# An eight-batch attention and feed-forward kernel on one core: odd pairs' reciprocals first in place 3, 512 KB transfers at other places, and the feed-forward part's first input taken as a ninth attention input

## What is computed

```python
x = x + _layernorm(_L0_attn_ref(_layernorm(x), w_q, w_kv, w_out, b_out, scale))   # 16 heads of 64
x = x + _layernorm(_L0_ffn_ref(_layernorm(x), w1, s1, w2, s2, h1, t1, h2, t2, w3, s3))

# attention: q, k of each head have their length set to 1; sim = exp(scale) * q k^T; softmax; times v; times w_out
# feed-forward: h = silu(x w1 * s1) * (x w2 * s2); h = gelu(h h1 * t1); h = gelu(h h2 * t2); h w3 * s3
```

## Time and profile before

| | us |
|---|---|
| median of three runs | 1770.43 |
| range of the three | 1767.59 to 1770.76 |
| the profiled execution, device time | 1771.34 |
| its span, first to last instruction | 1769.3 |
| attention: first scores to last scores (slots 0 to 255) | 35.4 to 1087.8 |
| first feed-forward matmul | 1104.2 |
| mean granted clock of TensorE | 0.991 |

### The profile page before, as it was taken

The page is one execution under the profiler, slowest core; times in us unless marked ns, Lnnn a source line. Parts: engine busy times, 40 slices in busy tenths (PEclk is TensorE's granted clock), DMA queues, the critical chain, the costliest instruction groups (busy, mean ns, idle before and its releaser), DMA issues.

```text
span 1769.3 us, 24636 instructions
## 1 busy us (share of the span) xinstructions
PE 1702.5 (96%) x8578; PEld 1421.8 (80%) x8578; DVE 1179.0 (67%) x2026; ACT 1010.0 (57%) x1350; POOL 463.4 (26%) x557
## 2 busy tenths in 40 slices
PE   5999999999999999999999998999999999999998
PEld 4778888888878887887888776888888888888887
DVE  5777877877877877877877775545454545445454
ACT  4876776877777776876877775323223231323231
POOL 3423543543533543543543331000000000000000
PEclk9999999999999999999999998999999999999999
DMA  4555556556656655655555665300000000000000
GB/s 132 128 127 142 128 134 146 128 134 146 138 126 144 137 132 138 137 129 130 114 116 130 160 150 127 140 12 4 22 24 1 25 1 24 1 24 1 24 1 24
DMA packets 76636, 162.89 MB, mean 92 GB/s; under 512 B 28256, under 2 KB 28640, under 8 KB 76512
## 3 DMA queue, kind: packets, MB, share of 16 engines
q1 hardware_dynamic: 67008, 127.59, 31.7%
q10 hardware_dynamic: 8496, 30.03, 5.7%
q0 software_dynamic: 1008, 3.67, 0.5%
HBM read 68.44 MB, written 20.19 MB: 50 GB/s over the span
## 4 chain that ended last, share of the span: by engine, by line
PE 78%; DVE 7%; DMA 5%; issue 4%; ACT 3%; POOL 1%; SPq 0%; ACTq 0%; DVEq 0%; POOLq 0%
PE bank L1059 16%; PE pair L1136 13%; PE pair L1137 12%; PE bank L1001 12%; PE bank L1073 5%; PE pair L1042 4%; PE pair L1043 4%; PE pair L1126 3%; PE pair L1127 3%; DVE Pl L716 2%; DMA work<-rows 2%; PE bank L1028 2%; DMA rows<-Rp 2%; PE bank L1153 2%; PE bank L1154 2%
## 5 line engine op out<-in xcount | busy, mean ns | idle before, releaser
L1059 PE MATMUL bank<-Ph,V 128*128 128x512 f32 x1024 | 371.1, 403 | 30.4 <-DVE Pl L716 29.1
L1136 PE MATMUL pair<-hh,f 128*128 128x512 f32 x1024 | 399.3, 390 | 0.7 <-DVE hl L829 0.2
L1137 PE MATMUL pair<-hl,f 128*128 128x512 f32 x1024 | 398.6, 389 | 0.0
L493 ACT ACTIVATE P<-pair,sh 128x1024 f32<-128x1024 f32 x256 | 286.5, 1119 | 179.0 <-PE pair L1043 145.9
L716 DVE TENSOR_TENSOR Pl<-P,Ph 128x1024 fp32r<-128x1024 f32 x256 | 314.2, 1227 | 1.4 <-ACT Ph L498 1.2
L550 ACT ACTIVATE hr<-pair,ct 128x512 f32<-128x512 f32 x128 | 88.3, 690 | 357.7 <-PE pair L1137 357.7
L1001 PE MATMUL bank<-w,xh 128*128 128x256 f32 (+1 forms) x1024 | 284.8, 340 | 5.5 <-DVE qk L695 2.3
L498 ACT ACTIVATE Ph<-P 128x1024 fp32r<-128x1024 f32 x256 | 271.8, 1062 | 8.1
L1059 PEld LDWEIGHTS bank<-Ph,V 128*128 128x128 f32 x1024 | 195.5, 191 | 92.6 <-issue 45.9
L1136 PEld LDWEIGHTS pair<-hh,f 128*128 128x128 f32 x1024 | 192.2, 188 | 43.8 <-DVE hl L829 3.4
L1137 PEld LDWEIGHTS pair<-hl,f 128*128 128x128 f32 x1024 | 192.2, 188 | 39.7
(11 more groups left out here) (104 smaller groups left out, 2652.0 us busy)
## 6 DMA issues: line engine op xcount, KB each, us to landing
stack<-turned SPq DMA_DIRECT2D x128, 384.0 KB, 4.4
stack<-turned SPq DMA_DIRECT2D x128, 256.0 KB, 4.7
work<-rows SPq DMA_DIRECT2D x128, 128.0 KB, 3.0
raw<-in_h ACTq DMA_DIRECT2D x16, 512.0 KB, 3.8
xr<-in_h ACTq DMA_DIRECT2D x16, 512.0 KB, 4.8
f<-raw ACTq DMA_DIRECT2D x12, 512.0 KB, 6.4
f<-raw SPq DMA_DIRECT2D x10, 512.0 KB, 7.5
xt<-in_x SPq DMA_DIRECT2D x8, 512.0 KB, 4.1
```

The costliest lines, as they stand in the source:

```text
L493: e.activation(M.P[:, i % 2, :], M.SB[i % 2][:, :], ACT.Exp, bias=M.sh[:, h:h + 1]).then_inc(S["exp"])
L1059: d = e.matmul(M.OB[:, :], v, p[:, u % 3, j * 512:(j + 1) * 512], start=jt == 0 and m == 0, stop=jt == 3 and m == 2)
L1136: e.matmul(ps, w, M.hh[src][:, k, :].bitcast(to), start=k == 0, stop=False)
L1137: d = e.matmul(ps, w, M.hl[src][:, k, :].bitcast(to), start=False, stop=k == KH - 1)
```

## The change

- **VectorE, place 3.** `invert` for odd pairs stands ahead of `p_low` instead of at the end of the slot. At place 7 it stays at the end.
- **VectorE, places 0 and 1.** `turn_low` for odd pairs moves from the end of place 0 to place 1, behind that slot's `p_low`.
- **VectorE, slot 21.** `normal` stands ahead of the second `x_low` and of `turn_low` instead of behind them.
- **Transfers.** The copies move from place 3 to place 7. The looks of slots 20 and 28 move to 21 and 29. `load_x` moves from slot 27 to slot 31, `load_xr` from 0 to 6 of the next batch, and `store_x1` ahead of the stack transfers of its slot. `LOADS` stays.
- **The flag.** `count_all` moves from slot 226 to 225, `flag_sum` on TensorE from 226 to 229, and `flag` from 227 to 230. `bank_plan` gives other banks from there on.
- **The ninth input.** The first feed-forward input goes the way of a batch's attention input: loaded at slot 223 into `xt`, normalized at slots 227 to 236 with half of that on GpSimd, transposed at 243 and 244, split at 245. The separate steps in slots 246 to 253 go. The tiles `xn`, `xh3`, `xl3` become the same memory as `xt`, `xh`, `xl`. The load of `xv` for the first batch moves behind the slots, to SyncE.

```diff
-FLAG_AT, BRANCH_AT = 226, NU - 1
+FLAG_AT, BRANCH_AT = 229, NU - 1
...
-LOOKS = (16,) + tuple(32 * b + r for b in range(7) for r in (20, 24, 28))
+LOOKS = (16,) + tuple(32 * b + r for b in range(7) for r in (21, 24, 29))
...
 def copy_at(i):
...
-    n, r = divmod(i - 11, 8)
+    n, r = divmod(i - 15, 8)
...
+        if 0 <= pb < B - 1 and i32_ == 16:
+            store_x1(pb)
         if pair_of(i) is not None:
             stack(pair_of(i), 0)
...
-        if b + 2 < B and i32_ == 27:
+        if b + 2 <= B and i32_ == 31:
             load_x(b + 2)
-        if i and i32_ == 0:
+        if 0 <= pb and i32_ == 6:
             load_xr(pb)
+    load_xv(0)
     load_xv(1)
...
-        if i == NU - 10:
-            load_xv0()
...
-        early = i % 4 == 1 and i32_ != 21
...
+        if r == 3 and 0 <= n - 2 < NP:
+            invert(n - 2)
         if 0 <= i - 1 < NU:
             p_low(i - 1)
+        if r == 1 and pair_of(i - 1) is not None:
+            turn_low(pair_of(i - 1), 1)
+            turn_low(pair_of(i - 1), 0)
...
-        if early and 0 <= n - 3 < NP:
+        if i % 4 == 1 and 0 <= n - 3 < NP:
             normal(n - 3)
...
-        if i % 4 == 1 and not early and 0 <= n - 3 < NP:
-            normal(n - 3)
-        if i % 4 == 3 and 0 <= n - 2 < NP:
+        if r == 7 and 0 <= n - 2 < NP:
             invert(n - 2)
...
-        if i == FLAG_AT:
+        if i == FLAG_AT - 4:
             count_all()
...
-        if i in (NU - 8, NU - 7):
-            norm3(0, 2 * (i - NU + 8))
-            norm3(0, 2 * (i - NU + 8) + 1)
...
-        if i // 32 + 1 < B and i % 32 in (19, 20):
+        if i < NU and i % 32 in (19, 20):
             x_turn(i // 32 + 1, i % 32 - 19)
-        if i == NU - 3:
-            turn3(0)
...
+        M.xn, M.xh3, M.xl3 = M.xt, M.xh, M.xl
```

More of the change, by code:

```diff
@@ L98, in bank_plan @@
             order += [(("y", 2 * quad_of(i)), i), (("y", 2 * quad_of(i) + 1), i)]
-        if b + 1 < B and i % 32 in (19, 20):
+        if b < B and i % 32 in (19, 20):
             order.append((("x", 2 * (b + 1) + i % 32 - 19), i))
-        if i == NU - 3:
-            order += [(("x3", 0), i), (("x3", 1), i)]
         if i == FLAG_AT:
@@ L140, in wait_bank @@
         elif kind == "x3":
-            q.wait_ge("xh3", n + 1)
-            q.wait_ge("xl3", n + 1)
+            q.wait_ge("xh3", n - 1)
+            q.wait_ge("xl3", n - 1)
     return bank
@@ L227, in load_x @@
             q.wait_ge("xT", 2 * b)
-        e.dma_start(M.xt[:, :, :], M.x[b]).then_inc(S["x"], 16)
+        if b == B:
+            q.wait_ge("x1", 16)
+        e.dma_start(M.xt[:, :, :], M.x[b] if b < B else M.x1[0]).then_inc(S["x"], 16)
     def load_wo(k):
@@ L408, in pool_program @@
         i32_, pb = i % 32, i // 32 - 1
-        if b + 1 < B and i32_ == 5:
+        if b < B and i32_ == 5:
             norm_root(b + 1)
@@ L412, in pool_program @@
             o_high(i // 4 - 2)
-        if b + 1 < B and i32_ in (5, 12):
+        if b < B and i32_ in (5, 12):
             for t in (0, 1) if i32_ == 5 else (2, 3):
@@ L532, in x3_high @@
             bank = PLAN["x3", 2 * b + k][0]
[L533 to L536, removed]
+            q.wait_ge("xT3", 2 * b + k - 1)
+            q.wait_ge("grp", grp(b - 1, 0, KH - 1))
             e.activation(M.xh3[:, k, :], M.TB[bank][:, :], ACT.Copy).then_inc(S["xh3"])
@@ L574, in act_program @@
         g, c, b, r, live = slot(i)
-        if b + 1 < B and i % 32 == 21:
+        if b < B and i % 32 == 21:
             x_high(b + 1, 0)
@@ L787, in norm3 @@
         q.wait_ge(f"x1{b % 2}", 16 * (b // 2 + 1))
-        q.wait_ge("xn3", NT * b)
-        stats(M.xv[:, b % 2, t, :], t, M.st, M.mv, "ln3", NT * b + t + 1)
+        q.wait_ge("xn", NT * (B + 1))
+        q.wait_ge("xn3", NT * (b - 1))
+        stats(M.xv[:, b % 2, t, :], t, M.st, M.mv, "ln3", NT * (b - 1) + t + 1)
         if t == NT - 1:
-            q.wait_ge("ln3b", NT * b + NT)
+            q.wait_ge("ln3b", NT * b)
             e.tensor_scalar_add(M.ve[:, :], M.mv[:, :, 1], EPS).then_inc(S["ve3"])
     def norm3b(b, t):
-        q.wait_ge("rd3", b + 1)
-        q.wait_ge("xT3", 2 * b)
-        free1(q)
+        q.wait_ge("rd3", b)
+        q.wait_ge("xT", 2 * B + 2)
+        q.wait_ge("xT3", 2 * (b - 1))
         e.tensor_scalar(M.xn[:, t, :], M.xv[:, b % 2, t, :], M.mv[:, t, 0:1], M.rd[:, t:t + 1],
@@ L878, in vector_program @@
         i32_, pb, n = i % 32, i // 32 - 1, i // 4 + 1
-        early = i % 4 == 1 and i32_ != 21
-        if b + 1 < B and i32_ == 21:
+        if b < B and i32_ == 21:
             x_low(b + 1, 0)
+        if r == 3 and 0 <= n - 2 < NP:
+            invert(n - 2)
         if 0 <= i - 1 < NU:
             p_low(i - 1)
+        if r == 1 and pair_of(i - 1) is not None:
+            turn_low(pair_of(i - 1), 1)
+            turn_low(pair_of(i - 1), 0)
         if i < 3:
@@ L906, in vector_program @@
             v_low(values_of(i))
-        if pair_of(i) is not None:
+        if r == 5 and pair_of(i) is not None:
             turn_low(pair_of(i), 1)
```

36 lines of the change are left out of this document (8 added, 28 removed).

## The result

The kernel after takes 1757.37 us (median of eight runs, 1754.84 to 1761.91), the kernel before 1768.12 in eight runs beside it: a ratio of 0.9942, 95% interval 0.9928 to 0.9956. It is faster by 10 us, where 25 were forecast. The profiled execution is the fastest of the eight: 1754.84 us, span 1753.0. The two spans so differ by 16.3 us, some 6 more than the medians do.

A forecast was written before the change was run, and what follows sets the result against it. Bound: TensorE, busy 1702.5 of 1769.3 us; only its attention waits and following 1.2 GHz stretches can move. Sum 14.3 + 0 + 1 + 3.8 + 7.5 − 1.5 = 25.1 us off 1771.3 gives 1746.2; range 1731 to 1763.

The forecast's parts named there:

- Slot 31: Earlier reciprocal and faster spread end VectorE's 3.21 us wait; seven slots 31 at 6.0 us each: 14.3 gained, ends 20.1, 7.3.
- Slot 21: Early `normal` ends TensorE's 0.46 us wait in slot 23, against a look beside a stack transfer: 0; ends 3.2 gained, 5 lost.
- `load_xr`: Its move from slot 0 to 6, with `store_x1` earlier: slot 5's `normal` waits less; 1 us gained, ends 0 and 2.5.
- sums late: Rival, chance 0.10: sums `Dp` are not there at place 3, so VectorE waits ahead of `p_low`; 15 gained, 1756 us.
- The copies: At place 7 they can slow the even pair's store or stack transfers; 0 taken, ends 0 and 11 us lost.
- So the copies cost nothing on this path: Even pair's store: in the last batch, beside a 512 KB load, it took 4.7 us and `normal` at place 1 did not wait.
- The end of 11: Worst end for the copies on the stack path: 22 × 0.5 = 11 us lost, where 0 was taken.
- `turn_low` at place 1: Low half put behind `p_low` delays the PSUM bank that `qk_tile` needs: 1.5 us lost, ends 0 and 13.
- 1.1 us of slack: Place 1: keys' first half done at 209.18, `qk_tile` starts at 210.27; the 1.1 us put ahead just use this up.
- The flag: TensorE's 2.13 us wait at slot 226 and 1.7 us of slow clock go: 3.8 us gained, ends 3.8 and 0.
- The ninth input: Batch 7 and hand-over: 2.3, 2.0 and 1.5 us of waits and 1.7 of slow clock go: 7.5 gained, ends 13 and 0.
- Slower rival: Chance 0.05: copy, look of slot 29 and `load_x` around one stack transfer at boundary 7 to 0; 1782 at 1.0 us each.

The follow-up runs named there:

- e7: The kernel before with one edit: `invert` for odd pairs first at place 3, ahead of the low half; 1750.72 us (0.9887).
- e10: The kernel before with odd pairs' `invert` first at place 3, `load_xr` at place 6, slot 21's `normal` early and the flag's move; 1741.21 us (0.9860).
- e6: e3 with looks, `load_x`, `load_xr` and `store_x1` back where the kernel before had them; 1751.56 us (0.9899).
- e2: The kernel after with the 22 copies back at place 3, all else as after; 1747.43 us (0.9881).
- e11: The kernel before with only the odd pairs' `turn_low` behind `p_low` at place 1 and the copies at place 7; 1778.82 us (1.0053).
- e14: e3 with the copies at place 5 in place of 3; 1748.47 us (0.9903).
- e4: The kernel before with the ninth input's edits alone, `load_x` for it at slot 219; 1769.54 us (0.9992).
- e9: e7 with one more edit: `load_xr` issued at place 6 of the batch in place of place 0; 1747.24 us (0.9879).
- e12: e3 with the last two of ScalarE's 512 KB `LOADS` in slots 254 and 255 in place of 250 and 251; 1740.89 us (0.9843).
- e3: The kernel after with odd pairs' `turn_low` back at place 0 and the copies back at place 3; 1740.52 us (0.9832).
- e1: The kernel after with odd pairs' `turn_low` back at place 0, copies left at place 7; 1751.84 us (0.9906).

## Why the prediction was right and wrong

Direction and range held (1757 lies in 1731 to 1763, and faster had 0.93). The forecast was 25 us of gain; 10 came by the medians, 16 between the two traces. That the range held is in part luck: slots 31, 23 and 22 gained 8 us more than forecast, which covers over half of what two parts cost.

- **Slot 31: −14.3 forecast, −20.0 measured.** The mechanism was right and the size was the far end. The cost that I took for the look of slot 29 on the stack transfer (6.0 a slot in place of 5.17) was not there: all seven are at the floor. e7 shows that the reciprocal's 3.9 us do it alone, and that moving the looks was not needed.
- **Slot 21: 0 forecast, −3.6 + 1.3 = −2.3 measured.** Slots 23 gained more than the 0.46 us that stood in the earlier trace rows. Slots 22 lost 0.18 each by the same kind of bank wait as place 1 (in slot 54 the weight load starts at 262.02, and the keys' low half has ended at 261.95), unforeseen. e10 has both without the rest.
- **`load_xr`: −1 forecast, for the wrong slots.** Slots 7 did fall by 1.9 us, but they fall as much in e6 and e7, where `load_xr` stays. Its worth is elsewhere: without the move the early reciprocal would have waited for its sums. The rival "sums late" thus did not come in after, since it had been forestalled, and came in e6 and e7, at 5 us.
- **The copies: 0 forecast, +7.3 in the trace, 10 us by e2.** The step that failed is "So the copies cost nothing on this path". It rested on one row of the last batch, where a store took 4.7 us and `normal` did not wait. That row nearly gave the price (5.7 in slot 87). That nobody waits was true of before's order on VectorE, and e11 finds it true there with the copies at place 7; it is not true of after's, where the store is closer behind and the spread falls behind the look. The end of 11 was in the range, though priced on the stack path, and there it is e14 that shows it.
- **`turn_low` at place 1: +1.5 forecast, +6.8 over 24 slots, some 8 to 9 in all.** The step that failed is "1.1 us of slack". I took the start of the first matmul for the moment from which TensorE waits. Its weight load stands 0.23 us earlier, which leaves 209.18 to 210.04, 0.86 us. The 1.1 us put ahead use this up in each group, and not in "four or so". Priced from the right row it is (1.1 − 0.86) × 32 = 7.7, which would have brought the forecast to 1752. The Trainium skill ("TensorE: Matmul & The Clock Gate", "Architectural detail: the array is 16× 32×32, not 1× 128×128") says that TensorE's queue can pull weight loads ahead of matmuls still in flight. The trace agrees: the load of 210.04 starts 0.23 us ahead of its matmul, while the one before it is still drawn as running (210.04 to 210.43).
- **The flag: −3.8 forecast, −4.1 measured** (15.63 to 11.49, clock 0.89 to 1.00).
- **The ninth input: −7.5 forecast, nothing by e4 and e10.** The step that failed took the waits before slot 251 and the slow clock for its gain. Batch 7 gained 3.7, no more than the flag's 4.1. (One trace does not settle this: slots 224 to 254 take 121.2 us in e4, without the flag's move, and 126.8 in e9, against 123.65 before. The medians of e4 and e10 do.) The waits for the last spreads stayed. I had named the two 512 KB loads beside them and not priced them; e12, which moves those two, gained nothing either. The 5.1 us behind slot 255 came in some kernels with and some without the ninth input.
- **Slower rival.** Copy, look and stack transfer side by side do cost as described, but in after the copy comes 3.3 us behind the two stack transfers for which the scores of place 0 wait. In slot 86 these took 3.8 and 4.7 us, 3.7 and 4.5 before, and came in time. e14 puts copy and look ahead of them, and pays 8.8 us.

The Trainium skill ("DMA: Bandwidth & Descriptors", "Issuing engines are not separate DMA queues") says that transfers started by ScalarE, SyncE or GpSimd all run on the same 16 DMA engines and interleave there. By that rule a change of place only picks whom a transfer slows. The runs agree: the copy slows the odd pair's spread at place 3 (4.5 us in slot 36 of e3, 2.8 in after, and nobody waits once the reciprocal is early), the even pair's store and the second head's stack transfers at place 7, and with a look the first head's at place 5. What decides is the slack of whoever is hit.

**The better kernel.** e3 takes 1740.52 us, 0.9832 of before, and e10 reaches 1741.21 with four small edits. They can't be told apart.

## What to carry over

Read the slack of a PSUM bank at the weight load of its next user, not at the matmul. Ask for the waits of the weight loads as well as for those of the matmuls, which all but leave such a wait out, and compare the length of all slots of a kind. Before moving a large transfer, find the small transfer within some 4 us behind it and ask who waits for that one after the change, not before. A part that is moved to help another edit is best tried alone: here one edit did more than all together, two parts cost 7 to 10 us each, and the largest, the ninth input, did nothing that shows.

## What the runs showed of the hardware

- In single transfers, a store of 4 KB took 1.7 us with nothing large within 4 us, 3.7 with a stack transfer 2.4 us ahead, 5.7 with one 2.2 us ahead and a 512 KB copy 3.1 us ahead on another engine's queue, and 2.7 where both were over 4 us ahead. One of 2 KB took 7.6 us behind a 512 KB load of its own queue, and 4.3 without.
- A wait of a weight load for a bank lengthened 24 slots by 6.8 us in sum, and the list of the matmuls' waits shows 0.2 us of it. The list for the weight loads has 30 waits, 12.7 us in sum.
- The same hand-over of 16.34 us ran at a granted clock of 1.00 in eight of the sixteen traces (after, e1, e2, e7, e9, e10, e12, e14) and at 0.69 to 0.90 in the other eight. From slot 255 to the end the first take 676 to 677 us, the others 679 to 683. The three kernels without early reciprocals (before, e4, e11) are all among the slower; of the thirteen with them, five are. One trace of each kernel can't say how much of this is chance.
